# Mamba-style scans cut in halves and started earlier in a fused decoder layer; softplus and layer norm moved between engines

## What is computed

```
x = x + attention(layernorm(x))           # 32 heads of 64, 8 key heads, rope, causal
x = x + ssm(context, gate=layernorm(x))   # below
x = x + ffn(layernorm(x))                 # 704 hidden, int weights minus 128, times scales

# ssm: 256 channels, 16 states, per batch a recurrence over the 256 tokens
u     = silu(causal_conv4(context @ in_proj) + conv_b)
dt, Bm, Cm = x_proj(u)
delta = softplus(dt_proj(dt) + dt_proj_b)
state = state * exp(delta * A) + (delta * u) * Bm
y     = (sum over the 16 states of state * Cm + D * u) * silu(z)
```

## Time and profile before

| | |
|---|---|
| time, median of 3 runs (lowest to highest) | 438.95 us (438.73 to 439.83) |
| the profiled execution: its time, its span | 438.5 us, 436.7 us |
| mean granted TensorE clock | 0.984 |
| busy share of the span: PE, PEld, DVE, ACT, POOL | 88%, 70%, 80%, 62%, 42% |
| chain that ended last: PE, DVE, issue, DMA, ACT, POOL | 39%, 18%, 17%, 11%, 6%, 6% |
| L832, 32 scans on DVE: busy, mean of one | 73.3 us, 2292 ns |
| L825, 32 drives on DVE: busy, mean of one | 41.3 us, 1292 ns |
| L838, 32 times_c on DVE: busy, mean of one | 38.6 us, 1205 ns |
| L510, 32 decays on ACT: busy, mean of one | 36.9 us, 1154 ns |

### The profile page before, as it was taken

One profiled execution on the slowest core, in us unless ns is written; L12 is line 12 of the kernel. 1 busy time (PEld: TensorE's weight loads), 2 busy tenths in 40 slices (PEclk: granted clock), 3 DMA queues, 4 the chain that ended last, 5 costly groups with the idle time before them and its releaser, 6 DMA issues.

```text
span 436.7 us, 7777 instructions
## 1 busy us (share of the span) xinstructions
PE 385.6 (88%) x2636; PEld 307.6 (70%) x2636; DVE 347.2 (80%) x479; ACT 268.8 (62%) x775; POOL 181.8 (42%) x262
## 2 busy tenths in 40 slices
PE   4879988999999988998899899988875999699996
PEld 2546776877887767786778677766664887488885
DVE  1766757888898998899989988998988998476532
ACT  2465799666776667666766666766653677543221
POOL 2653442355546254625562546354642453120000
PEclk9989999999999999999999999999999899889999
DMA  9852265358865679397656682965566942200000
GB/s 229 162 107 53 62 146 169 107 175 176 210 152 152 119 165 222 95 230 184 138 159 133 158 220 64 228 143 138 162 133 161 205 102 53 50 0 26 25 26 24
DMA packets 55431, 57.42 MB, mean 131 GB/s; under 512 B 32984, under 2 KB 43424, under 8 KB 55392
## 3 DMA queue, kind: packets, MB, share of 16 engines
q0 software_dynamic: 9792, 22.10, 25.1%
q1 hardware_dynamic: 35712, 28.44, 24.7%
q10 hardware_dynamic: 9888, 6.39, 5.1%
HBM read 26.36 MB, written 1.18 MB: 63 GB/s over the span
## 4 chain that ended last, share of the span: by engine, by line
PE 39%; DVE 18%; issue 17%; DMA 11%; ACT 6%; POOL 6%; SPq 2%; DVEq 0%; ACTq 0%; POOLq 0%
PE ps_p L1086 8%; DMA y<-state 6%; PE ps_so L1103 6%; PE ps_p L1313 5%; PE ps_so L1296 5%; PE ps_r L1155 4%; DVE nmax L745 4%; DVE state L825 4%; ACT prob L481 3%; POOL rc L403 3%; PE ps_p L1203 3%; DMA qt<-rc 2%; DMA bc<-bc_scratch 2%; DVE state L838 2%; PE ps_so L1114 2%
## 5 line engine op out<-in xcount | busy, mean ns | idle before, releaser
L481 ACT ACTIVATE prob<-ps_so,nmax 128x256 f32<-128x256 f32 (+1 forms) x256 | 104.7, 441 | 51.8 <-DVE nmax L745 51.7
L403 POOL TENSOR_TENSOR rc<-rc,rs 128x512 f32<-128x512 f32 x40 | 58.4, 1460 | 105.0 <-DVE rs L733 66.7
L832 DVE TENSOR_TENSOR_SCAN state<-decay,state 128x1024 f32<-128x1024 f32 x32 | 73.3, 2292 | 1.1
L487 ACT ACTIVATE pt<-ps_r 128x512 f32<-128x512 f32 x96 | 53.7, 593 | 31.6 <-PE ps_r L1155 31.6
L1086 PE MATMUL ps_p<-xt_all,wq 128*128 128x256 f32 x256 | 63.8, 392 | 9.9 <-DVE rs L737 4.9
L273 POOL DMA_DIRECT2D qt<-rc x128 | 65.0, 520 | 10.0 <-POOL rc L403 9.5
L745 DVE TENSOR_REDUCE nmax<-ps_so 128x2 f32<-128x512 f32 (+1 forms) x96 | 60.2, 683 | 10.5 <-PE ps_so L1114 10.5
L1086 PEld LDWEIGHTS ps_p<-xt_all,wq 128*128 128x128 f32 x256 | 46.2, 190 | 23.3 <-DVE rs L737 6.6
L1203 PE MATMUL ps_p<-wo,attn_t 128*128 128x256 f32 x256 | 60.9, 383 | 0.2 <-DVE attn_t L848 0.2
L410 POOL DMA_DIRECT2D y<-state x32 | 29.8, 932 | 73.1 <-DVE state L838 70.9
L481 ACT ACTIVATION_READ_ACCUMULATOR prob<-ps_so,nmax 128x1 f32 x256 | 57.9, 226 | 0.0
(11 more groups left out here) (108 smaller groups left out, 524.9 us busy)
## 6 DMA issues: line engine op xcount, KB each, us to landing
bc<-bc_scratch SPq DMA_DIRECT2D x32, 512.0 KB, 5.2
y<-state POOLq DMA_DIRECT2D x32, 512.0 KB, 5.9
qt<-rc SPq DMA_DIRECT2D x128, 32.0 KB, 2.4
qt<-rc POOLq DMA_DIRECT2D x128, 32.0 KB, 2.2
wo<-wo_t ACTq DMA_DIRECT2D x8, 256.0 KB, 4.3
wq<-wqkv_t SPq DMA_DIRECT2D x28, 64.0 KB, 2.5
kt<-kt SPq DMA_DIRECT2D x7, 256.0 KB, 3.0
kt<-rc POOLq DMA_DIRECT2D x34, 32.0 KB, 1.8
```

Of the source, the lines that this page charges most:

```text
L403: nc.gpsimd.tensor_tensor(rc[:, r % 2, :, :], rc[:, r % 2, :, :], rs[:], ALU.add).then_inc(rope_add, 1)
L481: nc.scalar.activation(o, i, ACT.Exp, bias=nmax[:, r, c:c + 1], accum_out=rsum[:, r, GRP + head:GRP + head + 1]).then_inc(exp_done, 1)
L487: nc.scalar.activation(pt[:, fill, :], ps_r[:, fill % 2, :], ACT.Copy).then_inc(pt_copied, 1)
L832: nc.vector.tensor_tensor_scan(state[:, v % 2, :], decay[:, v % 2, :], state[:, v % 2, :], 0.0, ALU.mult, ALU.add).then_inc(decay_free, 1)
```

## The change

A scan can now be done in halves of two batches (512 tokens), and the plan gives each unit from 3 to 30 two halves (one whole scan where they belong to the same v), and three in units 4, 6, 10, 14, 18, 22, 26 and 28. Worked out, the plan has these steps (f whole, a and b the halves): unit 3: 0f; 4: 1f, 2a; 5: 2b, 3a; 6: 3b, 4f; 7 to 9: 5f, 6f, 7f; 10: 8f, 9a; 11: 9b, 10a; 12: 10b, 11a; 13: 11b, 12a; 14: 12b, 13f; 15 to 17: 14f, 15f, 16f; 18: 17f, 18a; 19 to 21: 18b, 19a; 19b, 20a; 20b, 21a; 22: 21b, 22f; 23 to 25: 23f, 24f, 25f; 26: 26f, 27a; 27: 27b, 28a; 28: 28b, 29f; 29: 30a, 31a; 30: 30b, 31b. The last two scans are summed into `y` half by half, and gate_z of batches 0 and 1 waits for the first halves alone. In a unit with two steps of one half, both drives stand ahead of both scans, and both times_c follow the reciprocals; in a unit with three halves the first step goes there and the second one follows.

The softplus is done in units 0 to 2, in another order of steps, with 1 + e as a ScalarE copy with a bias; its last part (`finish_delta`, both blocks) stands after the reciprocals of unit 2. The layer norm of batches 1 to 3 is applied by GpSimd in its units 1 and 2; its statistics stay on VectorE and move into unit 0. ScalarE takes the two subtractions for the gate and up weights in units 11 and 15; those of the down weights move to units 9, 13, 21, 29 and 30, the statistics of x to units 17, 25 and 29. Except in units that project keys or values, ScalarE's exponentials for the next unit now follow both copies of the current one. The projections of `delta` (project_dt) move into unit 0.

```diff
-TWICE = (10, 14, 18, 22, 25, 26)
-SCANS = [0 if u < 5 or u == UNITS - 1 else 2 if u in TWICE else 1 for u in range(UNITS)]
+FIRST_SCAN = 3
+HALVES = [0 if u < FIRST_SCAN or u == UNITS - 1 else 3 if u in (4, 6, 10, 14, 18, 22, 26, 28) else 2
+          for u in range(UNITS)]
-DOWN_AT = (12, 16, 19, 20, 23, 24)
+DOWN_AT = {9: (0,), 13: (1,), 21: (2,), 29: (3,), 30: (4, 5)}
+X1_STATS_AT = {17: 0, 25: 1, 29: 2}
...
+def plan_scans():
+
+    v = 2 * NS
+    order = [(i, h) for i in range(v - 2) for h in range(2)] + [(i, h) for h in range(2) for i in (v - 2, v - 1)]
+    plan, at = [], 0
+    for n in HALVES:
+        steps = []
+        for i, h in order[at:at + n]:
+            if h and steps and steps[-1] == (i, 0, 1):
+                steps[-1] = (i, 0, 2)
+            else:
+                steps.append((i, h, h + 1))
+        plan.append(steps)
+        at += n
+    return plan
...
+def lead_scans(u):
+
+    return SCANS[u] if HALVES[u] < 3 else SCANS[u][:1]
...
+def sums_after(u):
+
+    done = []
+    for v, lo, hi in SCANS[u]:
+        if v >= 2 * NS - 2:
+            done.append((v, lo, hi))
+        elif hi == 2:
+            done.append((v, 0, 2))
+    return done
...
-                if u == 4:
+                if u == 3:
                     sp.wait_ge(ssm_ready, 5)
                     load_bc(1)
...
+            def add_y(v, lo, hi):
+
+                pool.wait_ge(hc_done, STEP_AT[v, hi - 1] + 1)
+                if sums_before(v, lo):
+                    pool.wait_ge(y_sum[v % 2], 16 * sums_before(v, lo))
+                cols = slice(lo * L // 2, hi * L // 2)
+                nc.gpsimd.dma_start(y[:, v % 2, cols], state[:, v % 2, cols], accum_op=ALU.add
+                                    ).then_inc(y_sum[v % 2], 16)
+
+            def ln_apply(b):
+
+                pool.wait_ge(ln_rstd, 2)
+                for i in range(b * TB, (b + 1) * TB):
+                    nc.gpsimd.tensor_scalar(x1[:, i, :], xs[:, i, :], mv[:, i, 0:1], rstd[:, i:i + 1],
+                                            ALU.subtract, ALU.mult).then_inc(ln_x, 1)
...
             for u in range(UNITS):
-                for v in scans(u - 1)[:1] if u else ():
-                    add_y(v)
+                for v, lo, hi in sums_after(u - 1)[:1] if u else ():
+                    add_y(v, lo, hi)
                 if u + 2 < UNITS:
                     add_rope(("q", u + 2))
                     move_q(nc.gpsimd, u + 2, range(GRP // 2, GRP), q_pool)
-                for v in scans(u - 1)[1:] if u else ():
-                    add_y(v)
+                for v, lo, hi in sums_after(u - 1)[1:] if u else ():
+                    add_y(v, lo, hi)
+                if u == 0:
+                    ln_rstds(1, B, 2)
+                if u == 1:
+                    ln_apply(1)
+                    ln_apply(2)
+                if u == 2:
+                    ln_apply(3)
...
+            def one_plus(e):
+
+                act.wait_ge(sp_e, 2 * e + 2)
+                nc.scalar.activation(state[:, e, :], decay[:, e, :], ACT.Copy, bias=1.0).then_inc(sp_w, 1)
...
+            def dequantise(i):
+
+                act.wait_ge(up_in if i else gate_in, 16 * 2)
+                nc.scalar.activation(wgu[:, i, :, :], wgu_i[:], ACT.Copy, bias=-ZERO_POINT).then_inc(wq_done, 1)
...
                 copy_pt(u, 0)
                 copy_pt(u, 1)
-                for v in scans(u)[:1]:
-                    decays(v)
-                if nxt:
+                for v, lo, hi in lead_scans(u):
+                    decays(v, lo, hi)
+                if u == 1:
+                    exp_delta(1)
+                late = u % KG in (1, 2) and u // KG + 1 < GROUPS
+                if late:
                     exps(u + 1, 2)
                 copy_pt(u, 2)
                 copy_rep(u)
+                if u == 3:
+                    copy_xt(2)
+                if nxt and not late:
+                    exps(u + 1, 2)
                 if nxt:
                     exps(u + 1, 1)
                     exps(u + 1, 0)
                 if u % KG == 2 and u // KG + 1 < GROUPS:
                     copy_v(u // KG + 1)
+                if u == 0:
+                    exp_delta(0)
                 if nxt:
                     widen(u + 1)
-                for v in scans(u)[1:]:
-                    decays(v)
-                if 1 <= u < B:
-                    copy_xt(u)
-                if u <= EB:
-                    prepare_scan(u)
+                for v, lo, hi in more_scans(u):
+                    decays(v, lo, hi)
+                if u == 0:
+                    one_plus(0)
+                if u == 1:
+                    one_plus(1)
+                    logs(0)
+                    logs(1)
+                if u == 2:
+                    copy_xt(1)
+                if u == 3:
+                    copy_xt(3)
+                if u in (11, 15):
+                    dequantise((11, 15).index(u))
...
-            dve.wait_ge(x_in[1], 16)
-            ln_stats(1, B)
-            ln_apply(1, B, 2)
             reciprocals(0)
...
+            def soften(e):
+
+                dve.wait_ge(sp_w, e + 1)
+                dve.wait_ge(sp_e, 2 * (e + 1))
+                then(nc.vector.scalar_tensor_tensor(decay[:, e, :], state[:, e, :], 1.0, decay[:, e, :],
+                                                    ALU.subtract, ALU.subtract))
+                then(nc.vector.scalar_tensor_tensor(delta[:, e, :], delta[:, e, :], 0.0, decay[:, e, :],
+                                                    ALU.max, ALU.subtract))
+
+            def finish_delta(e):
+
+                dve.wait_ge(sp_l, e + 1)
+                then(nc.vector.tensor_tensor(delta[:, e, :], delta[:, e, :], y[:, e, :], ALU.add))
+                dve.wait_ge(u_done, e + 1)
+                nc.vector.tensor_tensor(du[:, e, :], delta[:, e, :], u_s[:, e, :], ALU.mult
+                                        ).then_inc(ssm_ready, 1)
+                nc.vector.tensor_scalar(y[:, e, :], u_s[:, e, :], par[:, e, DC + 2:DC + 3], None, ALU.mult
+                                        ).then_inc(ssm_ready, 1)
...
+            def drive(v, lo, hi):
+
+                n, cols = v // 2, columns(lo, hi)
+                if v == 0:
+                    dve.wait_ge(ssm_ready, 5)
                 dve.wait_ge(bc_in[n % 2], (n // 2 + 1) * 32)
                 if v >= 2:
                     dve.wait_ge(y_sum[v % 2], 16 * (v // 2))
-                nc.vector.tensor_tensor(state[:, v % 2, :], du[:, v % 2, :], bc[:, n % 2, 0, :], ALU.mult
+                nc.vector.tensor_tensor(state[:, v % 2, cols], du[:, v % 2, cols], bc[:, n % 2, 0, cols], ALU.mult
                                         ).then_inc(drive_done, 1)
...
                 if u == 0:
                     add_dt(1)
+                    dve.wait_ge(x_in[1], 16)
+                    ln_stats(1, B)
                     add_dt(2)
...
+                if u in (1, 2):
+                    soften(u - 1)
+                for v, lo, hi in lead_scans(u):
+                    drive(v, lo, hi)
+                for v, lo, hi in lead_scans(u):
+                    scan(v, lo, hi)
                 if u % KG == 1 and u // KG + 1 < GROUPS:
                     rope(("k", u // KG + 1))
                 if u + 1 < UNITS:
                     reciprocals(u + 1)
-                for v in todo[:1]:
-                    times_c(v)
...
+                if u == 0:
+                    add_dt(3)
+                if u == 2:
+                    finish_delta(0)
+                    finish_delta(1)
+                for v, lo, hi in lead_scans(u):
+                    times_c(v, lo, hi)
+                for v, lo, hi in more_scans(u):
+                    drive(v, lo, hi)
+                    scan(v, lo, hi)
+                    times_c(v, lo, hi)
+                for i in DOWN_AT.get(u, ()):
+                    dequantise_down(i)
+                if u in X1_STATS_AT:
+                    x1_stats(X1_STATS_AT[u], X1_STATS_AT[u] + 1)
...
             def gate_z(b):
 
+                for e in range(EB):
+                    dve.wait_ge(y_sum[e], 16 * (NS if b < B // 2 else NS + 1))
```

178 lines of the change are left out of this document (66 added, 112 removed).

## The result

The changed kernel takes 446.35 us (median of 4 runs, 444.8 to 447.59), the kernel before took 439.21 beside it (438.73 to 439.83): a ratio of 1.0165, 95% interval 1.0139 to 1.019. It is 7 us slower. The prediction said 439.4, no change that can be measured, in a range from 432 to 447.

The account below looks back on a forecast made before the run. From unit 9 on, VectorE's list (its work plus the waits inside it) was taken to bound the kernel. 438.5 + 7.8 (start) - 4.9 (units 5 to 30) - 2.0 (end) = 439.4 us, range 432 to 447.

Parts of the forecast that it names:

- part 6: Start, units 1 to 4: logarithms and both finish_delta delay unit 3 to 73.5 and unit 5 to 92.8, +7.8 us.
- parts 1 and 2: Units 5 to 30: six second scans become half scans, -3.9 us; ten units with paired halves cost +2.0 us.
- part 3: Units 5 to 30: VectorE's waits for sums into y grow from 8.4 to 12.8 us, 5.6 in unit 29; +4.4.
- part 5: Units 5 to 8, 29 and 30: waits on TensorE vanish once VectorE is behind, -5.6 us.
- 7, the end: After the scans: gate_z of batch 0 no longer waits 4.25 us for the last sum, -2.0 us.
- rival (d): Start: GpSimd's four normalising instructions take 1.6 us each, unit 2 starts 4 us later, 443.4 us; chance 0.12.
- parts 1, 2 and 4: Half-scan terms (-3.9, +2.0), and gate and up subtractions taken off VectorE in units 5 to 30, -1.8 us.
- (c): Sums land late: each of eight close pairs waits 2 to 4 us, half of these counted, 447.5 us; chance 0.15.
- (a): Sums land early, 4.5 us each: small waits vanish, unit 29 waits 1 us less, 432.4 us; chance 0.17.
- (b): Units 6, 14, 22 and 28: half leads are cheap, 12 us not 13.6; -5.7, 433.7 us; chance 0.12.
- (e): The end: something else holds gate_z, so ending by batch pairs does not help, 441.4 us; chance 0.08.

Follow-up runs that it names:

- e6: Changed kernel, but gate_z of every batch waits for all sums again: 445.39 us (4 runs), ratio 1.0152 to the kernel before.
- e10: Changed kernel, but in unit 2 both finish_delta stand ahead of the reciprocals of unit 3: 443.66 us (4 runs), ratio 1.0118 to the kernel before.
- e9: Changed kernel, but in unit 1 GpSimd adds and moves the keys before normalising batches 1 and 2: 445.5 us, ratio 1.0147 to the kernel before.
- e3: Changed kernel, but GpSimd issues the sum of scan 29 ahead of unit 29's rotation add and moves: 442.64 us, ratio 1.0052 to the kernel before.
- e4_nosums: Changed kernel without any of the transfers that add the states to y: 431.46 us (one run).
- e2: Changed kernel with scans planned as before (whole from unit 5, last two in halves): 441.13 us (8 runs), ratio 1.0094 to the kernel before.

## Why the prediction was right or wrong

The table puts the prediction's steps against the profiles (us). "Idle" is VectorE's.

| part | predicted | measured | |
|---|---|---|---|
| 6, start of unit 5 | +7.8 | +9.0 | of it +6.4 from unit 1 on |
| 6, start of unit 3 | 73.5 | 73.65 | |
| 1, units 6, 14, 22 | 13.6 | 13.9, 13.6, 13.6 | idle 2.17 each |
| 1, units 10, 18, 26 | 12.0 | 11.8, 11.9, 11.9 | |
| 1, unit 28 | 12.4 | 11.8 | idle 0.83 |
| 2, a pair of halves | +0.2 a unit | 0 | unit 12: 8.3 |
| 3, unit 29's sum | 5.6 | 5.5 | |
| 3, all other sums and broadcasts | 7.2 | 8.3 | sums 1.7, broadcasts 6.6 |
| 5, waits on TensorE | -5.6 | +4.6 at L836 | |
| units 5 to 30 | -4.9 | +1.2 | |
| 7, the end | -2.0 | -3.0 | 2.1 by e6, at like clock |

**The start (part 6)** was right in mechanism and nearly in size. ScalarE's two logarithms and second table load set unit 3, and the finish_delta stood behind an idle 2.16 us, which e10 shows to be on the path. That unit 3 was met to 0.15 us is in part luck: unit 1 came 2.6 us later and not 1.6, in the scatter of the profiles, and from there to unit 3 were 0.8 less than forecast. In unit 4 VectorE then waits 0.99 us for a sum, at 91.33, which no part had priced. The first half of rival (d) happened: GpSimd's four products took 1.42 us each, near its upper price of 1.6, and held unit 2 up for 3.4 us. Its step from unit 2 to unit 3 was wrong, as e9 shows.

**The halves (parts 1 and 2)** were priced well, their pairs too high. The timeline of unit 12 shows that a pair cost as much as a whole scan (8.3 us for the unit, as the whole one in unit 3), with the two drives 0.6 apart though each lasts 0.68:

```profile
176.35 1.28 DVE L911 TENSOR_TENSOR state<-du,bc 128x512 f32<-128x512 f32 x2
177.55 2.33 DVE L919 TENSOR_TENSOR_SCAN state<-decay,state 128x512 f32<-128x512 f32 x2
179.80 0.17 DVE L845 RECIPROCAL rinv<-rsum 128x8 f32<-128x8 f32 x1
179.89 1.24 DVE L926 TENSOR_TENSOR state<-state,bc 128x512 f32<-128x512 f32 x2
181.05 0.68 DVE L823 TENSOR_TENSOR rc<-ps_p,cos_s 128x512 f32<-128x512 f32 x1
```

VectorE: DVE Perf Modes of the Trainium skill (the errata section) has a fixed latency on each instruction; adding it up gives 0.16 us more for a pair, an estimate. Its 691 ns for 512 columns agrees with the 0.68 of one, but back to back the second starts under the first (1.28 us for the two drives), and the trace decides for no extra in the unit.

**The sums (part 3)** were half right. The wait of unit 29 came to within 0.2 us, and e3 shows it whole on the path. The close pairs were overrated: 0.9 us at 186.18 in unit 13 where 2.4 were taken, none over 0.6 in units 20 and 21. Their place was taken by broadcasts, which the prediction left out as a term of its own: 2.11 us in unit 8 and 4.49 in unit 24. Its steps added up the sums' landing times but not the broadcasts', which lie in the same stretch.

**The failed step is the account of lateness, in parts 3 and 5.** Without its 12.8 us of waits the prediction has 282.0 - 12.8 = 269.2 us for units 5 to 30. e4_nosums, the same work with little left to be late, takes 271.5, one wait of 4.8 us for scores among it. So parts 1, 2 and 4 and the slack of part 5 were right within some 2.5 us, a little low with that wait and a little high without it. From there to the changed kernel's 288.05 are 16.6 us, 3.8 more than the 12.8; together the 6.1 that were missing. With +1.2 at the start and -1.0 at the end they make up the distance from 439.4 to the profiled 445.64. What failed is the premise of part 5, that once VectorE is behind, it never waits for TensorE. VectorE was behind, yet its waits at the maxima grew from 6.3 to 10.9 us, as TensorE stood waiting for query moves (10.7 us on `qt<-rc` in four places of units 5 to 30, the longest 4.6). TensorE's list has landing times in it too, which the prediction never priced. Of the three long ones (3.14, 1.23 and 4.10 us) the first falls into full DMA engines. DMA: Bandwidth & Descriptors of the Trainium skill ("Issuing engines are not separate DMA queues") says that transfers of all issuing engines run on the same 16 DMA engines and interleave there; the trace agrees, as the eight moves of 32 KB issued from two engines at 129 to 132 us landed after 6.2 to 7.6 us (median of all: 2.2) with the share at 1.0. The third has another cause beside it (last section).

**Why the kernel before suffers less** is argued, not shown. The bytes are the same in both (57.42 MB), and in units 5 to 30 the mean share of the DMA engines is lower after (0.61 against 0.66), yet taking the sums away gives the kernel before 5 us and the changed one 14. A likely reason is that the kernel before had its slack in the right places: where VectorE waited 1.26 us for a rotation's add in most key units, a move or a sum could be as late for nothing. Which slack hid which transfer was not tried.

**The rivals.** The measured time is near that of (c), 447.5, but its mechanism was not: the sums landed no later (median 5.5 us after, 5.9 before) and the close pairs waited little. The upper end of the range, 447, was set by (c) alone, so that 446.35 lies inside it is luck. (a) came half true: the waits of the close pairs nearly went (1.7 us for 7.2), though a sum took over its 5.0 us, and unit 29 waited in full; broadcasts and query moves took more than was saved. (b) did not happen: the half leads idled their 2.17 us. (e) did not either, but the 3.0 us of the two profiles overstate the end, as its granted clock was 0.95 before and 1.00 after; the changed ending at 0.95 takes 64.6 and 65.1 us (e2 and e4), no less than the 64.9 before. The 2.1 us against e6 are the fair size.

**Slips in the sums.** None moves the forecast by more than 0.2 us. Unit 5 adds up to 92.65 and not 92.8. Rival (b) adds up to -5.2 and not -5.7 (three units of 1.6, and 0.4 in unit 28), so 434.2. Part 3's 9.8 us for the tile of 31a takes a landing of 4.9 us that no row has (4.55 and 6.58 do); the tile came at 9.7.

## What to carry to other kernels

Work taken off the engine that is behind turns into time only as far as nothing else lands just in time: here 8.9 us less of VectorE work came with 10.1 us more of waiting. Before counting such a gain, list every transfer whose landing the tighter list would meet (the moves that feed another engine too, not only those the busy engine waits for now), and try the kernel with one kind of traffic left out; that gives the price of lateness. Before two profiles of one stretch are compared, compare their granted clocks. And a step that starts sooner should stand ahead of the wait that comes next in its list: the half leads, the late sum of 29 and finish_delta each cost 2 to 5 us by their place alone. With whole scans and finish_delta moved the same idea is 1% faster than the kernel before.
